# All steps of a gated delta-rule kernel in a new order on five engines, and GpSimd's state operands in three steps

## The reference

```python
kn = k_t / max(norm(k_t), 1e-12)
pred = einsum('bhji,bhj->bhi', S, kn)
r = clip(v_t - pred, -1, 1)
S = a_t[..., None] * S
kp = einsum('bhd,bhde->bhe', kn, S)
S = S + b_t * kn[..., None] * (v_t - kp)[..., None, :]
o = einsum('bhji,bhj->bhi', S, q_t)
R = aR_t[..., None] * R
kpR = einsum('bhd,bhde->bhe', kn, R)
R = R + g_t * kn[..., None] * (r - kpR)[..., None, :]
o = o + einsum('bhji,bhj->bhi', R, q_t)
```

## Time and profile before

| | |
|---|---|
| median of three runs | 2300.88 us (2300.46 to 2311.26) |
| profiled execution, its own time | 2300.65 us |
| its span | 2298.4 us |
| mean granted TensorE clock | 0.975 |
| TensorE, VectorE busy | 94%, 80% |
| ScalarE, GpSimd busy | 45%, 56% |

### The profile page before, as it was taken

The page is one execution under the profiler, slowest core; times in us unless marked ns, Lnnn a source line. Parts: engine busy times, 40 slices in busy tenths (PEclk is TensorE's granted clock), DMA queues, the critical chain, the costliest instruction groups (busy, mean ns, idle before and its releaser), DMA issues.

```text
span 2298.4 us, 114374 instructions
## 1 busy us (share of the span) xinstructions
PE 2156.6 (94%) x49472; PEld 1843.1 (80%) x49472; DVE 1839.2 (80%) x3728; ACT 1028.8 (45%) x2137; POOL 1287.1 (56%) x2384
## 2 busy tenths in 40 slices
PE   7999987999999999999998999999998999999988
PEld 3454545888888888888888888989887888888887
DVE  5501025799999899989998999999997999999974
ACT  3333245444444444444444444454443444444420
POOL 0010014666667656666667776676666666667651
PEclk9999998799999999999999999999999999999997
DMA  3000001222222223222223222222222223333331
GB/s 93 0 1 0 21 1 32 68 64 67 67 66 68 68 67 69 67 67 67 67 67 78 55 63 65 67 67 67 64 67 70 67 70 72 72 72 72 72 72 28
DMA packets 336176, 134.91 MB, mean 59 GB/s; under 512 B 285504, under 2 KB 324544, under 8 KB 335680
## 3 DMA queue, kind: packets, MB, share of 16 engines
q1 hardware_dynamic: 334480, 125.24, 23.2%
q10 hardware_dynamic: 1200, 2.36, 0.3%
HBM read 66.69 MB, written 60.82 MB: 55 GB/s over the span
## 4 chain that ended last, share of the span: by engine, by line
PE 53%; POOL 14%; DMA 12%; SPq 8%; DVE 7%; issue 6%; ACT 1%; POOLq 0%; DVEq 0%; ACTq 0%
POOL lane_x L1226 7%; POOL lane_t L1223 7%; SPq L312 4%; PE bank L582 4%; PE bank L419 4%; PE bank L432 4%; DMA lane_n<-n_dram 4%; DMA x_dram<-lane_x 4%; PE bank L610 3%; PE bank L601 3%; DMA n_dram<-AR 3%; SPq L302 2%; PE bank L631 2%; PE bank L504 2%; PE bank L622 2%
## 5 line engine op out<-in xcount | busy, mean ns | idle before, releaser
L1223 POOL TENSOR_TENSOR lane_t<-lane_n,lane_x 128x15 f32<-128x15 f32 (+7 forms) x960 | 337.3, 351 | 491.5 <-DMA lane_n<-n_dram 421.4
L582 PE MATMUL bank<-kq,Kt 64*64 64x96 f32 x8192 | 374.1, 233 | 23.2 <-issue 18.2
L1226 POOL TENSOR_TENSOR lane_x<-lane_x,lane_t 128x15 f32<-128x15 f32 (+7 forms) x960 | 336.1, 350 | 75.2
L582 PEld LDWEIGHTS bank<-kq,Kt 64*64 64x64 f32 x8192 | 324.3, 135 | 30.7 <-issue 29.9
L1427 ACT ACTIVATE dk<-bank 128x512 f32<-128x512 f32 x64 | 38.2, 597 | 489.5 <-PE bank L601 489.5
L1419 ACT ACTIVATE kend<-Kt,ek 128x64 f32<-128x64 f32 x768 | 189.5, 335 | 0.0
L939 DVE TENSOR_TENSOR_SCAN cum<-rst,dk 128x512 f32<-128x512 f32 x128 | 159.7, 1249 | 19.3 <-ACT dk L1375 19.3
L990 DVE COPY_PREDICATED AS<-cst,bank 128x384 f32<-128x384 int32 x256 | 148.8, 581 | 0.5 <-PE bank L582 0.5
L687 PE MATMUL bank<-yS,AS 64*64 64x64 f32 x2048 | 134.5, 223 | 9.2 <-DVE Sst L1034 5.1
L1198 POOL TENSOR_TENSOR KQF<-efull,q 128x768 f32<-128x768 f32 x64 | 141.9, 2217 | 0.0
L881 DVE TENSOR_TENSOR dn<-bank,s3b 128x512 f32<-128x512 f32 x8 | 5.5, 690 | 169.7 <-PE bank L444 169.7
(11 more groups left out here) (163 smaller groups left out, 6254.6 us busy)
## 6 DMA issues: line engine op xcount, KB each, us to landing
k_dram<-kend SPq DMA_DIRECT2D x64, 384.0 KB, 2.5
kend_in<-k_dram SPq DMA_DIRECT2D x256, 96.0 KB, 2.2
XF<-x_dram SPq DMA_DIRECT2D x256, 64.0 KB, 2.3
lane_n<-n_dram SPq DMA_DIRECT2D x128, 124.0 KB, 2.8
x_dram<-lane_x SPq DMA_DIRECT2D x128, 124.0 KB, 2.5
n_dram<-AS SPq DMA_DIRECT2D x256, 32.0 KB, 1.7
n_dram<-AR SPq DMA_DIRECT2D x256, 32.0 KB, 1.7
wt<-in_win SPq DMA_DIRECT2D x4, 640.0 KB, 4.5
```

Source lines behind the costliest of these rows:

```text
L582: ins = pe.matmul(v3(dst[hd[h], o:o + kinds * C], kinds)[:, :, i * SUB:(i + 1) * SUB], Kt[hd[h], m * 96 + i * SUB:m * 96 + i * SUB + C], r ...
L1223: pool.tensor_tensor(tv, lane_n[:, m * SUB + m + 1:m * SUB + BASE].unsqueeze(2).to_broadcast([L, rows, m + 1]), xv[:, m, 0:m + 1].unsqueez ...
L1226: pool.tensor_tensor(xv[:, m + 1:, 0:m + 1], xv[:, m + 1:, 0:m + 1], tv, ALU.subtract).then_inc(s["lane_step"], 1)
```

## The change

The five `body` functions are reordered. In TensorE's and VectorE's the end of one body and the beginning of the next are moved across the border as well (level 0 of a quad is now at the end of TensorE's body k, chunk 1's state at the end of VectorE's), so a line can have another k at the same place in the cycle. `against_state` becomes `against_k`, `against_q` and `against_prev`, with a semaphore `qf` of its own for q. No arithmetic is added or removed.

The diff without its first hunk, which adds the text of `qf`:

```diff
@@ -342,7 +342,6 @@
     def body(k):
         b, l = on(k + 2), on(k + 1)
         if l:
-            keys_in(k + 1)
             lanes_out(k + 1)
         if 0 < k + 4 <= LAST and (k + 4) % B == 0:
             load_weights(k + 4)
@@ -353,8 +352,10 @@
         if b:
             blocks_out(k + 2, 0)
             blocks_out(k + 2, 1)
+            lanes_in(k + 2)
             keys_out(k + 2)
-            lanes_in(k + 2)
+        if l:
+            keys_in(k + 1)
     load_weights(0)
@@ -748,20 +749,10 @@
         ins.then_inc(s["out_ps"], 1)
     def body(k):
-        a, b, l, e, f = on(k + 3), on(k + 2), on(k + 1), on(k - 1), on(k - 2)
-        if f:
-            s_s(k - 2, 2)
-            r_s(k - 2, 1)
-        if e:
-            level0_nx(k - 1)
-        if f:
-            s_o(k - 2, 2)
-            s_p(k - 2, 2)
-        if e:
-            level0_zd(k - 1)
+        a, b, l, d, e, f = on(k + 3), on(k + 2), on(k + 1), on(k), on(k - 1), on(k - 2)
         if f:
             s_w(k - 2, 3)
-            r_o(k - 2, 1)
+            s_o(k - 2, 2)
             r_w(k - 2, 2)
             s_y(k - 2, 3)
         if l:
@@ -772,23 +763,24 @@
         if e:
             level1_nx(k - 1)
         if b:
-            project_v(k + 2)
+            norms(k + 2)
         if e:
             level1_zd(k - 1)
         if b:
-            norms(k + 2)
+            project_v(k + 2)
+        if f:
+            s_o(k - 2, 3)
+        if e:
+            s_y(k - 1, 0)
         if f:
             r_s(k - 2, 2)
-            r_o(k - 2, 2)
-        if e:
-            s_y(k - 1, 0)
-        if f:
-            s_o(k - 2, 3)
-            r_w(k - 2, 3)
-        if e:
-            s_s(k - 1, 0)
         if l:
             products(k + 1, 1)
+        if e:
+            s_s(k - 1, 0)
+        if f:
+            r_w(k - 2, 3)
+            r_o(k - 2, 2)
         if e:
             s_p(k - 1, 0)
         if f:
@@ -807,28 +799,37 @@
         if e:
             s_o(k - 1, 0)
             s_s(k - 1, 1)
-            r_s(k - 1, 0)
         if l:
             products(k + 1, 4)
         if e:
-            r_o(k - 1, 0)
+            r_s(k - 1, 0)
             s_p(k - 1, 1)
...
             r_w(k - 1, 1)
+            r_o(k - 1, 0)
             s_w(k - 1, 2)
-            s_o(k - 1, 1)
-            r_y(k - 1, 1)
-            s_y(k - 1, 2)
-        if a:
-            project_k(k + 3)
-            project_q(k + 3)
         if f:
             project_out(k - 2)
         if a:
+            project_q(k + 3)
             project_a(k + 3)
+            project_k(k + 3)
             project_r(k + 3)
+        if e:
+            s_y(k - 1, 2)
+            r_y(k - 1, 1)
+            s_o(k - 1, 1)
+            s_s(k - 1, 2)
+            r_s(k - 1, 1)
+        if d:
+            level0_nx(k)
+        if e:
+            r_o(k - 1, 1)
+            s_p(k - 1, 2)
+        if d:
+            level0_zd(k)
     for k in range(-3, LAST + 3):
@@ -1079,46 +1080,37 @@
     def body(k):
         a, b, l, d, e, f = on(k + 3), on(k + 2), on(k + 1), on(k), on(k - 1), on(k - 2)
         if e:
-            s_state(k - 1, 1)
-        if l:
-            mask_products(k + 1, 3)
-        if e:
-            r_state(k - 1, 0)
-        if l:
-            mask_products(k + 1, 4)
-        if e:
             s_clip(k - 1, 1)
         if l:
             scale_blocks(k + 1, 0)
-        if e:
-            r_right(k - 1, 1)
-            s_right(k - 1, 2)
-        if l:
             mask_products(k + 1, 5)
             scale_blocks(k + 1, 1)
-        if e:
-            s_solved(k - 1, 2)
-            r_solved(k - 1, 1)
         if b:
             operands_k(k + 2)
+        if e:
+            s_right(k - 1, 2)
+            r_right(k - 1, 1)
         if f:
             add_out(k - 2)
         if b:
-            operands_prev(k + 2)
+            operands_q(k + 2)
+        if e:
+            s_solved(k - 1, 2)
+            r_solved(k - 1, 1)
         if d:
             turn_inverse(k)
+        if b:
+            operands_prev(k + 2)
         if e:
             s_state(k - 1, 2)
         if b:
-            operands_q(k + 2)
-        if e:
-            r_state(k - 1, 1)
+            own_half(k + 2)
+        if e:
             s_clip(k - 1, 2)
-        if b:
-            own_half(k + 2)
         if a:
             clamp_s(k + 3)
         if e:
+            r_state(k - 1, 1)
             s_right(k - 1, 3)
         if d:
             level0(k)
@@ -1127,36 +1119,37 @@
             s_solved(k - 1, 3)
         if d:
             turn_level0(k)
+        if a:
+            clamp_r(k + 3)
+        if d:
+            turn_keys(k)
         if e:
             r_solved(k - 1, 2)
         if a:
-            clamp_r(k + 3)
             running_sums(k + 3, 0)
+            running_sums(k + 3, 1)
         if e:
             s_clip(k - 1, 3)
-        if a:
-            running_sums(k + 3, 1)
         if d:
-            turn_keys(k)
             level1(k)
-        if e:
-            r_state(k - 1, 2)
-        if d:
-            s_solved(k, 0)
-        if b:
-            mask_products(k + 2, 0)
-        if e:
-            r_right(k - 1, 3)
-        if d:
-            s_state(k, 0)
         if a:
             norm_k(k + 3)
         if d:
-            s_clip(k, 0)
-        if e:
-            r_solved(k - 1, 3)
+            s_solved(k, 0)
+        if e:
+            r_state(k - 1, 2)
+        if b:
+            mask_products(k + 2, 0)
+        if d:
+            s_state(k, 0)
+        if e:
+            r_right(k - 1, 3)
         if b:
             mask_products(k + 2, 1)
+        if d:
+            s_clip(k, 0)
+        if e:
+            r_solved(k - 1, 3)
         if d:
             s_right(k, 1)
         if b:
@@ -1166,6 +1159,13 @@
             s_solved(k, 1)
         if a:
             from_anchors(k + 3)
+        if d:
+            s_state(k, 1)
+        if b:
+            mask_products(k + 2, 3)
+            mask_products(k + 2, 4)
+        if d:
+            r_state(k, 0)
     for k in range(-3, LAST + 3):
@@ -1180,24 +1180,35 @@
         pool.tensor_tensor(v3(dk[:, 4 * T:6 * T], NM), cm[:, :, 0:SUB], anchor.to_broadcast([P, NM, SUB]), ALU.subtract)
         pool.tensor_tensor(v3(dk[:, 6 * T:], NM), anchor, cm[:, :, C - 1:C], ALU.subtract).then_inc(s["dfar"], 1)
-    def against_state(n):
-        r = n % RING
+    def state_cols(n):
+        return v4(KQF[n % RING][:, :], 5, 2), v4(efull[:, :], 2, 2)
+
+    def late(t):
+        return v3(t[:, :], 2)[:, :, C:].unsqueeze(1).to_broadcast([P, 2, 2, T - C])
+
+    def against_k(n):
         need(pool, "e_full", n + 1)
         need(pool, "kn", n + 1)
+        need(pool, "o_ps", n - RING + 1)
+        if n == 2:
+            pool.wait_ge(s["ffn_added"], GROUPS)
+        kv, ef = state_cols(n)
+        pool.tensor_tensor(kv[:, KF_S:KF_R + 1:3], ef, late(kn), ALU.mult).then_inc(s["kf"], 1)
+
+    def against_q(n):
+        need(pool, "e_full", n + 1)
         need(pool, "q_sb", n + 1)
         need(pool, "o_ps", n - RING + 1)
         if n == 2:
             pool.wait_ge(s["ffn_added"], GROUPS)
-        kv = v4(KQF[r][:, :], 5, 2)
-        ef = v4(efull[:, :], 2, 2)
-
-        def late(t):
-            return v3(t[:, :], 2)[:, :, C:].unsqueeze(1).to_broadcast([P, 2, 2, T - C])
-
-        pool.tensor_tensor(kv[:, KF_S:KF_R + 1:3], ef, late(kn), ALU.mult).then_inc(s["kf"], 1)
-        pool.tensor_tensor(kv[:, QF_S:QF_R + 1:3], ef, late(q), ALU.mult)
+        kv, ef = state_cols(n)
+        pool.tensor_tensor(kv[:, QF_S:QF_R + 1:3], ef, late(q), ALU.mult).then_inc(s["qf"], 1)
+
+    def against_prev(n):
         need(pool, "kf", n + 1)
+        need(pool, "qf", n + 1)
         need(pool, "ea1", n + 1)
+        kv, ef = state_cols(n)
         pool.tensor_tensor(kv[:, KP_S], v3(ea1[:, :], 2), kv[:, KF_S], ALU.mult).then_inc(s["kfull"], 1)
     def far_half(n):
@@ -1228,8 +1239,10 @@
     def body(k):
         a, b, l = on(k + 3), on(k + 2), on(k + 1)
         if b:
-            against_state(k + 2)
+            against_q(k + 2)
             far_half(k + 2)
+            against_k(k + 2)
+            against_prev(k + 2)
         if l:
             small_inverses(k + 1)
         if a:
@@ -1445,14 +1458,14 @@
             gate(k + 3, 0)
             copy_q(k + 3)
             squares(k + 3)
+            gate(k + 3, 1)
             log_decay(k + 3, 0)
-            gate(k + 3, 1)
             log_decay(k + 3, 1)
         if d:
             level1(k)
         if a:
+            norms(k + 3)
             copy_v(k + 3)
-            norms(k + 3)
             from_begin(k + 3)
         if e:
             copy_out(k - 1)
@@ -1460,8 +1473,8 @@
             to_end(k + 2)
         if a:
             from_anchor(k + 3)
+            gate_inverse(k + 3)
             to_anchor(k + 3)
-            gate_inverse(k + 3)
     load_ln_exp()
```

(4 more changed lines are left out.)

20 lines of the change are left out of this document (11 added, 9 removed).

## The result

After the change the kernel takes 2389.8 us (median of four runs, 2387.56 to 2398.89); the kernel before took 2300.81 us on the same chip (four runs, 2300.46 to 2311.26). The ratio is 1.0383, with an interval of 1.0343 to 1.0423. That is 89 us slower, where I forecast 2280 and gave "slower" 0.23; it lies outside the range as well. The profiled execution of after took 2391.26 us (span 2389.0) at a mean granted clock of 0.98.

The account below looks back on a forecast made before the run. The prediction took PE, DVE and the lane loop as balanced to within a microsecond. It summed 2300.65 - 22 (lane loop) + 2 (`keys_in`, once) = 2280.7 us and predicted 2280 us, range 2228 to 2335.

Parts of the forecast that it names:

- slower: Sign of the whole result: kernel time beyond the 0.5% limit, above 2312.4 us; chance 0.23.
- The lane loop: GpSimd's lane steps: one collision with DVE fewer, -0.7 us a step over 32 of 64 steps, 22 us gained.
- DVE's holds: DVE instructions held by GpSimd: nothing taken; bounds +0.7 and -1.8 us a step.
- the walk: GpSimd's and DVE's new orders followed from the lane steps' end: holds of 3.5 us a step, old order 2.8.
- PE's order: Projections ahead of s_y 2, r_y 1 and s_o 1: 0; bounds -7 us over the run, +0.5 us a step.
- slower, by the holds: Rival: the walk's +0.7 us a step, less PE's slack, costs about 25 us, giving 2326 us; chance 0.09.
- SP's `keys_in`: Issued later in SP's queue, delaying DVE before `turn_keys`: zero a step, 2 us once; upper bound 0.9 us a step.
- the slow rival: DVE's wait for `keys_in` before `turn_keys` reaches PE: 2358 us, at half of it 2330; chance 0.15.
- ACT's swaps: ScalarE's reordered instructions cost nothing, as ACT is busy for 45% of the span.

Follow-up runs that it names:

- a_sp_old: The changed kernel with SP's old queue order, `keys_in` first and `lanes_in` after `keys_out`: 2342.24 us, ratio 1.0216.
- a_dve_first: The changed kernel with VectorE's `s_right` 2 and `r_right` 1 ahead of `operands_k`, `s_solved` 2 and `r_solved` 1 ahead of `operands_q`: 2309.24 us, ratio 1.0072.
- a_gp_short: The changed kernel with GpSimd's three multiplications against the state cut to 2 of 192 columns from quad 4 on, order and waits kept: 2267.66 us, ratio 0.987.
- a_gp_old: The changed kernel with GpSimd's four steps back in the order k, q, previous, far half: 2306.34 us, ratio 1.0054.
- b_gp_new: The kernel before with only GpSimd's steps in the new order q, far half, k, previous: 2295.99 us, ratio 1.0002.
- a_sp_gp_old: The changed kernel with both SP's and GpSimd's old orders: 2290.98 us, ratio 0.9966.
- b_pe_dve_new: The kernel before with the new orders of TensorE and VectorE alone; ScalarE, SP and GpSimd in their old orders: 2385.56 us, ratio 1.0383.
- a_dve_old: The changed kernel with VectorE's old order alone, the other engines as changed: 2406.78 us, ratio 1.0496.

## Why the prediction was wrong, point by point

**The lane loop, -22 us.** Its mechanism was right as far as it went: in the step shown the long lane steps are two (1.27 and 1.10 us, under the scans) where three stood before, `far` runs freely in 1.08 us, and the loop has slack (in that step SP has fetched XF by 1516.63 and waits until 1518.38 for `scale_blocks` 0). But it gained nothing: another loop had become the longer one.

**DVE's holds, 0 with +0.7 us a step as the bound.** The sum of the walk was near, in part by luck: at the medians the four instructions `scale_blocks` 0 and 1, `operands_k` and `from_anchors` are held for 0 + 1.0 + 1.6 + 1.1 = 3.7 us, where the walk said 3.5 for `operands_q` in place of `from_anchors`. Of its own four it is 2.7 us, since `operands_q` is held for 0.1 and not 1.05. VectorE's busy time rose by 1.04 us a step, somewhat more than the bound. Their places were wrong. The walk let the far half begin at 3.05 after the lane steps, without asking when ek is ready. It waits for ScalarE, 267.2 us in 62 places, and so k against the state, not the far half, falls on `operands_k`. That is an omission in the walk: I followed two engines and left out the third that feeds them.

The Trainium skill ("SBUF — State Buffer", section "Who interferes with whom") says that the order of issue decides which of the two blocks. The rows agree: q against the state starts at 1512.67 and runs its usual 1.81 us, and the `from_anchors` of 1513.21 takes 2.36; the `operands_k` of 1520.65 starts under k against the state (to 1522.40) and takes 2.83, of which 1.75 are the overlap; previous, started under `operands_k`, takes 1.87 where 1.00 is its shortest. What no reading of that rule alone gives is the price: GpSimd's new order brings holds in both kernels (to a mean of 2219 ns for `operands_k` in before, 2694 in after), and costs nothing in the one and 76 us in the other.

**PE's order, 0 with +0.5 us a step as the bound. This is the step that failed.** I wrote that s_s 2 "now comes 1 us behind s_y 2, with `s_solved` 2 queued behind `operands_q` on DVE", and charged half of that microsecond. I priced the wait and did not walk the loop around it. (The saving of that paragraph was real: TensorE's wait for `wR` fell from 20.3 to 0.5 us.) The time of the projections before s_y 2 is not slack for VectorE: VectorE fills it with two scale steps, `operands_k`, `add_out` and `operands_q`, all ahead of `s_solved` 2. From `s_right` 1 to `s_solved` 2 it needs 13.3 us, every hold included, where it needed 7.96 in that step and 8.4 at the median, and PE's part, 16.4 us where nothing disturbs it (the usual step of a_sp_old, 30.0, less 13.6, with `s_solved` 2's own 0.3), follows in series. With a_dve_first `operands_q` leaves this stretch and `s_right` 2 no longer stands behind `operands_k`: it is 11.7 us, and 72 us of the run are back with most of the holds in place. With a_gp_short or a_gp_old it is 10.7 or 12.1 us by shorter holds, and 118 or 76 us are back with VectorE's order in place. Both are needed for the loss: b_gp_new has the one without the other (1.0002), a_sp_gp_old the other without the one (0.9966). The rival "slower, by the holds" had the sign and half of the mechanism, at 25 us of 89: it let PE's slack absorb the holds, which in this loop it did not. The two are no terms that add up, and my sum, which treated them as such, could not have found them.

**SP's `keys_in`, zero a step.** The wait before `turn_keys` that I worked out (1.9 us a step) hardly came in after: 5.8 us in the whole run, since VectorE reaches `turn_keys` later than I had it. There the slow rival named the right DMA and the wrong victim. The cost in after, 38 us, comes with TensorE standing without instructions just after `lane_n`, `k_dram` and `kend_in` crowd the DMA engines. It stands at `level0_zd`, which is inside the PE half of the loop above, so it lengthens the step in full; the records show 24.7 us of it against 3.0, and 22.6 us more in PE's busy time, a third of it by the clock. Where the loop is shorter, SP's order costs less: 20 us with GpSimd's order old (1.0054 and 0.9966), 13 us with `s_right` and `s_solved` first (1.0072 and 1.0016). The pauses are gone there, and the wait that I worked out appears instead: 15.0 us in a_gp_old, 9.9 in a_dve_first and 51.6 in a_gp_short, and none where SP's order is the old one.

**ACT's swaps, nothing.** True of ACT's load, wrong as a rule: two of its instructions sit on others' waits. ek ahead of the gate's inverse was worth 22 us in after, and the norms ahead of `copy_v` were needed by VectorE's new order (all of ScalarE's swaps together: 96 us between b_pe_dve_new and a_sp_gp_old).

**What stays open.** PE's order alone was not run, so it has no share of its own here; a_dve_old shows how much a misfit between PE's and VectorE's orders can cost. That the burst delays TensorE's instructions is argued, not shown, and some 15 of the 22.6 us in PE's busy time are not assigned to anything.

## What to carry to other kernels

Before moving work ahead of an instruction, ask whether that instruction closes a loop between two engines, and add up the loop: all of the one engine's stream between the two instructions, holds included, and all of the other's on the way back. A hold, or a GpSimd operation that waits, costs little as long as it isn't in the tightest such loop, and close to its full length in every step once it is, until another loop is the longer one. When an order written by hand is changed, follow each input of a moved instruction to the engine that makes it, even an engine that is idle for half of the time.

## What the runs showed of the hardware

- VectorE and GpSimd hold each other in both directions, for the rest of the instruction that started first: 1.28 us of work took 2.36, 1.22 took 2.83, and on GpSimd 1.00 took 1.87. Over a whole run this moved VectorE's busy time between 1728.6 us (a_gp_short) and 1915.3 us (a_sp_old) with the same 3728 instructions, and busy time does not tell the run's time: a_dve_old has 1794.9 us and is the slowest of all.
- Where two engines were in a loop, the steps tended to one length: 31 of 63 steps of b_pe_dve_new took 30.8 us and 27 of a_sp_old 30.0 us, where before's most frequent value, 28.8, comes 9 times.
- TensorE stood up to 2.0 us with nothing to wait for just after a burst in which DMA share reached 0.92; `keys_in` back at its old place in SP's queue took the total at that line from 24.7 to 3.0 us. 33 of the 35 such pauses of over 0.5 us in after's recurrence ended 1.2 to 1.7 us after a 16 KB packet of the instruction queue.
- After six of the nine such pauses of 1.2 to 2.0 us at `level0_zd`, TensorE's granted clock was at the lower level (0.50) for 3.4 to 6.8 us.
